# A gated cross-attention layer: the prologue's projections, remainders and bounds in another order

## The reference

```
x = x + tanh(g_xattn) * attention(layernorm(x), ctx, Wq, Wk, Wv, Wo, bo)   # 16 heads of 64
x = x + tanh(g_ffn)  * (layernorm(x) @ W[idx] + b[idx])
q = xn @ Wq ; k = ctx @ Wk ; v = ctx @ Wv
attention = softmax(q @ k.T * 64**-0.5) @ v, heads joined, @ Wo + bo
idx = argmax(log_softmax(logits) - log(-log(u)))     # one of 8 ffn matrices
```

## Time and profile before

| | |
|---|---|
| median of three runs | 1044.47 us |
| profiled execution | 1044.38 us |
| its span, first to last instruction | 1042.6 us |
| granted TensorE clock | full speed over the whole span |
| PE busy | 1027.6 us, 99% |
| DVE busy | 848.2 us, 81% |
| ACT busy | 746.9 us, 72% |
| POOL busy | 442.4 us, 42% |
| between 45 and 88 us: PE, ACT, POOL, DVE busy | 38.49, 37.42, 39.09, 31.66 us of 43 |

### The profile page before, as it was taken

One profiled execution on the slowest core, in us unless ns is written; L12 is line 12 of the kernel. 1 busy time (PEld: TensorE's weight loads), 2 busy tenths in 40 slices (PEclk: granted clock), 3 DMA queues, 4 the chain that ended last, 5 costly groups with the idle time before them and its releaser, 6 DMA issues.

```text
span 1042.6 us, 21852 instructions
## 1 busy us (share of the span) xinstructions
PE 1027.6 (99%) x6074; PEld 587.2 (56%) x6074; DVE 848.2 (81%) x1800; ACT 746.9 (72%) x2720; POOL 442.4 (42%) x637
## 2 busy tenths in 40 slices
PE   9998999999999999999999999999999999999997
PEld 7634455555555555555555555555555555555555
DVE  4678988888888888888888888888888887888876
ACT  3788877777677667776677677776776677767761
POOL 1586344444443344444433344444433344444422
PEclk9999999999999999999999999999999999999999
DMA  8513566666566665665566666655566656655655
GB/s 313 120 31 94 107 124 127 142 123 128 112 133 137 138 136 123 141 128 114 115 135 136 139 135 129 142 119 111 125 137 136 136 129 135 137 119 111 133 107 142
DMA packets 383073, 135.02 MB, mean 130 GB/s; under 512 B 361930, under 2 KB 362750, under 8 KB 382974
## 3 DMA queue, kind: packets, MB, share of 16 engines
q1 hardware_dynamic: 382974, 134.09, 59.4%
HBM read 27.48 MB, written 16.78 MB: 42 GB/s over the span
## 4 chain that ended last, share of the span: by engine, by line
PE 89%; DVE 4%; ACT 3%; DMA 2%; SPq 1%; issue 1%; POOL 0%; DVEq 0%
PE banks L1407 82%; PE banks L1640 3%; ACT work L905 1%; PE banks L1517 1%; DMA fold_area<-in_L_xattn_Wo 1%; PE banks L1453 1%; PE banks L1525 1%; PE banks L1506 1%; DVE fold_area L1124 1%; DVE work L449 1%; ACT vw_area L849 0%; DMA work<-work 0%; DVE vw_area L1113 0%; DVE red L1033 0%; DVE work L1211 0%
## 5 line engine op out<-in xcount | busy, mean ns | idle before, releaser
L905 ACT ACTIVATE work<-banks,red,cst 128x77 f32<-128x77 f32 x1024 | 408.9, 425 | 83.3 <-DVE red L1202 83.2
L1407 PE MATMUL banks<-fold_area,work 128*128 128x456 f16 (+1 forms) x2304 | 405.4, 335 | 2.6 <-DMA work<-work 1.9
L1407 PE MATMUL banks<-vw_area,work 128*128 128x512 f16 x1674 | 371.4, 379 | 1.0 <-DMA work<-work 1.0
L1407 PEld LDWEIGHTS banks<-fold_area,work 128*128 128x128 f16 x2304 | 225.2, 98 | 171.1 <-DMA work<-work 2.7
L1407 PEld LDWEIGHTS banks<-vw_area,work 128*128 128x128 f16 x1674 | 163.6, 98 | 186.1 <-DMA work<-work 1.9
L449 DVE SCALAR_TENSOR_TENSOR work<-work 128x256 f16<-128x256 f32 (+3 forms) x443 | 241.0, 578 | 0.8 <-ACT work L928 0.3
L905 ACT ACTIVATION_READ_ACCUMULATOR work<-banks,red,cst 128x1 f32 x1024 | 219.5, 214 | 0.0
L1200 DVE TENSOR_REDUCE stats<-banks 128x6 f32<-128x462 f32 (+1 forms) x192 | 112.0, 583 | 103.1 <-PE banks L1407 102.7
L1407 PE MATMUL banks<-work 128*128 128x256 f16 x1302 | 162.4, 272 | 0.7 <-DVE work L1287 0.5
L1407 PEld LDWEIGHTS banks<-work 128*128 128x128 f16 x1302 | 126.9, 98 | 31.9 <-DVE work L1287 0.7
L732 POOL TENSOR_TENSOR stats<-stats,cst 128x1 f32<-128x1 f32 x64 | 12.5, 196 | 282.4 <-DVE stats L1236 282.4
(11 more groups left out here) (150 smaller groups left out, 817.8 us busy)
## 6 DMA issues: line engine op xcount, KB each, us to landing
work<-in_x SPq DMA_DIRECT2D x64, 256.0 KB, 2.8
out<-work SPq DMA_DIRECT2D x63, 256.0 KB, 2.2
work<-work SPq DMA_TRANSPOSE x253, 3.1
fold_area<-in_L_xattn_Wo SPq DMA_DIRECT2D x4, 512.0 KB, 9.4
work<-in_L_ffn_W SPq DMA_DIRECT2D x2, 1024.0 KB, 8.3
fold_area<-in_L_xattn_Wq SPq DMA_DIRECT2D x2, 1024.0 KB, 14.2
fold_area<-in_L_xattn_Wv SPq DMA_DIRECT2D x3, 512.0 KB, 6.3
fold_area<-in_L_xattn_Wk SPq DMA_DIRECT2D x2, 768.0 KB, 12.4
```

The lines of the kernel that those rows point to most:

```text
L905: nc.scalar.activation(probs_of(place, place + 1), s_heads(m, k)[:, h - h0, :], ACT.Exp, bias=nmx[:, h:h + 1], scale=exp_scale, accum_out= ...
L1407: mm = nc.tensor.matmul(ps, lhs(l), rhs(r), start=first and n == 0, stop=last and n == 2, skip_group_check=onto)
```

## The change

The order of the visits in the first half of the key phase is another one. All four projections stand first, then two remainders, then the spread and the first turn; KEY 0 to 3 are folded before remainders 2 and 3. From KEY 8 on, and with the same banks, the list is as before. SPREAD becomes two visits: 0 for KK and WQ, 1 for WF. The bounds change engines: of the query matrix, ACT takes the first half in two passes and DVE the second in one reduction; the ffn matrix goes from one reduction on DVE to two passes on ACT. The pieces for x stand at later visits.

```diff
-        FROM = [0, 6, 11, 16, 21]
-        PARTS = [5, 4, 4, 4, 1]
+        FROM = [0, 6, 11, 16, 20]
+        PARTS = [5, 4, 4, 3, 2]
...
-        VISITS = [(PROJECT, 0), (PROJECT, 1), (PROJECT, 2), (REMAINDER, 0), (VALUE, 0), (PROJECT, 3), (REMAINDER, 1), (VALUE, 1),
...
+        VISITS = [(PROJECT, 0), (PROJECT, 1), (PROJECT, 2), (PROJECT, 3), (REMAINDER, 0), (REMAINDER, 1), (SPREAD, 0), (TURN, 0),
+                  (VALUE, 0), (KEY, 0), (KEY, 1), (VALUE, 1), (TURN, 1), (KEY, 2), (KEY, 3), (VALUE, 2), (REMAINDER, 2), (SPREAD, 1),
+                  (KEY, 4), (KEY, 5), (VALUE, 3), (REMAINDER, 3), (TURN, 2), (KEY, 6), (VALUE, 4), (KEY, 7), (VALUE, 5), (PASS, 0), (VALUE, 6),
...
# POOL
-                if (kind, n) == (REMAINDER, 1):
+                if (kind, n) == (KEY, 3):
                     x_scale(0, 0)
-                if (kind, n) == (KEY, 7):
+                if (kind, n) == (KEY, 11):
                     x_scale(0, 1)
...
# ACT
+            def ffn_bounds():
+
+                act.wait_ge(wf_loaded, 16)
+                for n, junk in enumerate((wv_raw[:, CT - 1, :], fold_area[:, A_WORDS + CT * ID:A_WORDS + CT * ID + ID])):
+                    rows = wf_raw[:, n * KT // 2:(n + 1) * KT // 2, :].rearrange("p k n -> p (k n)")
+                    nc.scalar.activation(junk, rows, ACT.Abs, accum_out=part_of(WF, n)).then_inc(parts_ready[WF], 1)
...
             copy_k(0)
+            copy_k(1)
             act.wait_ge(scale_v_ready, 1)
...
                 if t == 0:
-                    act.wait_ge(parts_ready[WF], 1)
+                    act.wait_ge(parts_ready[WF], PARTS[WF])
...
+                if (kind, n) == (PROJECT, 2):
+                    query_bounds()
+                if (kind, n) == (PROJECT, 3):
+                    ffn_bounds()
...
-                if (kind, n) == (VALUE, 2):
+                if (kind, n) == (VALUE, 3):
                     x_normalized(0, 0)
-                if (kind, n) == (REMAINDER, 3):
+                if (kind, n) == (KEY, 6):
                     x_high(0, 0)
...
# DVE
             largest(VV)
+            key_part(0)
             power_of_two(VV, 3)
...
-            dve.wait_ge(wf_loaded, 16)
-            part(WF, 0, wf_raw)
-            largest(WF)
-            key_part(0)
             key_part(1)
...
+                if (kind, n) == (PROJECT, 2):
+                    dve.wait_ge(wq_loaded[1], 16)
+                    part(WQ, 0, wq_raw[:, KT // 2:KT, :])
+                    largest(WQ)
...
-                if (kind, n) == (PROJECT, 3):
+                if (kind, n) == (KEY, 1):
+                    largest(WF)
                     x_moments(0, 0)
                     dve.wait_ge(x_stats, 1)
                     x_variance()
-                if (kind, n) == (KEY, 1):
+                if (kind, n) == (KEY, 7):
                     x_low(0, 0)
...
-                if (kind, n) == (KEY, 4):
+                if (kind, n) == (KEY, 8):
                     x_moments(0, 1)
...
# PE
-                if (kind, n) == (PROJECT, 0):
+                if (kind, n) == (PROJECT, 1):
                     spread(VV, 3)
```

More of the change, by code:

```diff
@@ L364, in flamingo_layer @@
         PROJECT, REMAINDER, VALUE, SPREAD, TURN, KEY, PASS = range(7)
-        VISITS = [(PROJECT, 0), (PROJECT, 1), (PROJECT, 2), (REMAINDER, 0), (VALUE, 0), (PROJECT, 3), (REMAINDER, 1), (VALUE, 1),
-                  (SPREAD, 0), (TURN, 0), (REMAINDER, 2), (VALUE, 2), (REMAINDER, 3), (KEY, 0), (KEY, 1), (VALUE, 3), (TURN, 1),
-                  (PASS, 0), (KEY, 2), (KEY, 3), (VALUE, 4), (PASS, 1), (KEY, 4), (KEY, 5), (VALUE, 5), (TURN, 2), (KEY, 6), (KEY, 7), (VALUE, 6),
+        VISITS = [(PROJECT, 0), (PROJECT, 1), (PROJECT, 2), (PROJECT, 3), (REMAINDER, 0), (REMAINDER, 1), (SPREAD, 0), (TURN, 0),
+                  (VALUE, 0), (KEY, 0), (KEY, 1), (VALUE, 1), (TURN, 1), (KEY, 2), (KEY, 3), (VALUE, 2), (REMAINDER, 2), (SPREAD, 1),
+                  (KEY, 4), (KEY, 5), (VALUE, 3), (REMAINDER, 3), (TURN, 2), (KEY, 6), (VALUE, 4), (KEY, 7), (VALUE, 5), (PASS, 0), (VALUE, 6),
                   (KEY, 8), (KEY, 9), (VALUE, 7), (TURN, 3), (KEY, 10), (KEY, 11), (VALUE, 8), (KEY, 12), (KEY, 13), (VALUE, 9),
@@ L807, in copy_k, with query_bounds @@
                                banks[:, pair_of(PROJECT, n):pair_of(PROJECT, n) + 2, 0:BS]).then_inc(k_copied, 1)
-            def query_bounds(half):
+            def query_bounds():
                 act.wait_ge(floor_set, 1)
-                act.wait_ge(wq_loaded[half], 16)
+                act.wait_ge(wq_loaded[0], 16)
                 act.wait_ge(v_done, HP)
-                for k in (2 * half, 2 * half + 1):
-                    nc.scalar.activation(wv_raw[:, k, :] if k < CT else fold_area[:, A_WORDS + CT * ID:A_WORDS + CT * ID + ID], wq_raw[:, k, :],
-                                         ACT.Abs, accum_out=part_of(WQ, k)).then_inc(parts_ready[WQ], 1)
+                for k in range(KT // 2):
+                    nc.scalar.activation(wv_raw[:, k, :], wq_raw[:, k, :], ACT.Abs, accum_out=part_of(WQ, 1 + k)).then_inc(parts_ready[WQ], 1)
+            def ffn_bounds():
[3 more added lines that the diff above has]
+                    nc.scalar.activation(junk, rows, ACT.Abs, accum_out=part_of(WF, n)).then_inc(parts_ready[WF], 1)
             copy_k(0)
+            copy_k(1)
             act.wait_ge(scale_v_ready, 1)
@@ L871, in _ @@
             for kind, n in VISITS:
-                if kind == PROJECT and n > 0:
+                if kind == PROJECT and n > 1:
                     copy_k(n)
+                if (kind, n) == (PROJECT, 2):
+                    query_bounds()
+                if (kind, n) == (PROJECT, 3):
+                    ffn_bounds()
                 if kind == REMAINDER:
@@ L877, in _ @@
                     value_high(n)
[L878 to L881, removed]
                 if kind == KEY:
@@ L1168, in _ @@
                     key_part(n)
+                if (kind, n) == (PROJECT, 2):
+                    dve.wait_ge(wq_loaded[1], 16)
+                    part(WQ, 0, wq_raw[:, KT // 2:KT, :])
+                    largest(WQ)
                 if (kind, n) == (PROJECT, 3):
                     largest(KK)
-                    largest(WQ)
-                if kind == SPREAD:
+                if (kind, n) == (SPREAD, 1):
+                    power_of_two(WF, pair_of(SPREAD, 1))
+                if (kind, n) == (SPREAD, 0):
                     first = pair_of(SPREAD)
@@ L1179, in _ @@
                                                    op0=ALU.mult, op1=ALU.mult).then_inc(scale_q_ready, 1)
-                    power_of_two(WF, first, P)
-                if (kind, n) == (PROJECT, 3):
+                if (kind, n) == (KEY, 1):
+                    largest(WF)
                     x_moments(0, 0)
@@ L1488, in taken_before @@
                 elif kind == SPREAD:
-                    for m in (KK, WQ, WF):
+                    for m in (WF,) if n else (KK, WQ):
                         pe.wait_ge(pow_step[m], 1)
@@ L1546, in _ @@
                     value_unit(n)
-                if kind == SPREAD:
-                    spread(WF, pair_of(SPREAD), P)
+                if (kind, n) == (SPREAD, 1):
+                    spread(WF, pair_of(SPREAD, 1))
+                if (kind, n) == (SPREAD, 0):
                     spread(KK, pair_of(SPREAD))
```

## The result

| | before | after |
|---|---|---|
| median of 22 runs each, side by side | 1044.01 us | 1045.54 us |
| ratio | | 1.0014, 95% interval 1.0009 to 1.0020 |
| profiled execution / its span | 1044.38 / 1042.6 us | 1045.01 / 1043.2 us |
| KEY 0 folds | 45.42 | 39.92 |
| VALUE 8 folds | 63.77 | 65.06 |

The changed kernel is slower by 1.5 us, 0.14%. The forecast was 1045.4, a change of +1.0. KEY 0 folds 5.5 us earlier, and 25 us later all of it is gone and 1.3 us more. In the profile the exponentials begin 1.29 us later and the spans differ by only 0.6: before's profiled execution had one longer wait for a transpose near its end, 1.20 us where the changed kernel has 0.57. Whether the other executions had it isn't known; their medians differ by 1.5.

A forecast was written before the change was run, and what follows sets the result against it. PE fills 130 to 1000 us, so only its start moves; DVE, POOL and the ffn reload tie the fold phase. 0.0 (POOL) + 0.97 (DVE and ACT) = +1.0 on 1044.38: 1045.4 us, own range 1044.2 to 1046.4, wider range 1042.6 to 1047.2.

The forecast's parts named there:

- What bounds: Whole kernel: PE fills 130 to 1000 us, so only its start moves; no single engine fills the fold phase before.
- The ties of DVE and POOL: End of fold phase: value 7's low half on DVE precedes VALUE 8's fold; POOL's splits run nearly without a gap.
- The reload's: Tie of the ffn matrix, requested when POOL's last value split ends; exponentials follow its two uses, forecast at 92.2 us.
- To the first key fold: Walk from the projections to KEY 0: it folds at 39.55 against 45.42, 5.9 us early, but owed on PE.
- the meeting for x_low: Remainder 3 on POOL: two small subtractions meet DVE's x_low and take 1.39 us; without it the sum is 0.5 smaller.
- POOL: Deciding term: first split 2.3 us late, idle 2.33, remainder 3 ends 59.54, free for VALUE 12 at 75.18; price 0.0.
- The long form of remainder 3's subtractions: POOL's two small subtractions in remainder 3 again take 1.39 us, against 0.94 in remainder 2.
- DVE: Second moments and ACT's wait ahead of value 7's low half: VALUE 8 folds at 64.74 against 63.77, 0.97 us late.
- What I cost at nothing: Moves priced at zero: later x_low(0,0), SP's transposes and bias rows 8 us later, the WF spread and its steps.
- the head start's 1041.9: First rival: ACT's work fills the phase, 5.9 us gained and 3.4 owed, so 2.5 us faster; chance 0.14.
- No change: Second rival: DVE's idle 0.52 and a hardly waiting VALUE 6 copy swallow the moments, 1044.4 us; chance 0.22.
- POOL later than VALUE 12's copy: Third rival: idle before KEY 3 grows, POOL free for VALUE 12 after about 76.2; 1047.2 at 2.8 late; chance 0.16.

The follow-up runs named there:

- e1: Changed kernel with the second tile's moments on DVE behind KEY 6 instead of KEY 8; ratio 1.0011 to the kernel before.
- e2: Changed kernel with remainder 3's split ahead of VALUE 3's split on POOL; ratio 1.0010 to the kernel before.
- e6: Changed kernel with the two remainder stages exchanged, so VALUE 6 shares room with remainders 0 and 2, order unchanged; ratio 1.0009 to the kernel before.
- e4: Kernel before with the second tile's moments behind KEY 8 and its four short POOL instructions behind KEY 11; ratio 1.0002 to the kernel before.
- e5: Kernel before with only the bounds' change of engines, visits as before; ratio 1.0002 to the kernel before.
- e3: Changed kernel with the first tile's moments and POOL's four short instructions back at their old places; ratio 1.0012 to the kernel before.
- e8: Changed kernel with remainder 2 ahead of KEY 0, stages exchanged, first x pieces at old places, second moments, x_low and x_high moved; ratio 0.9994 to the kernel before.

## Why the prediction was right

- *The number*: the mechanism held, the closeness of 1045.4 to 1045.54 is partly luck. The starting point of 1044.38 was 0.37 above the median of 22 runs, and the change was +1.5 against +1.0.
- *What bounds*: the stretch behind 130 us kept its shape and began 1.31 us later, and the exponentials moved with value 7's low half. The ties of DVE and POOL held. The reload's was loose by a hair: its uses ended at 92.34 and DVE's maxima at 92.45, so in the changed kernel the chain runs through the folds.
- *To the first key fold*: forecast 39.55, measured 39.92. One step more than covers the 0.37, the product that makes the query scale. Before it took 0.16 us; now 0.62. It began at 37.75 and ended at 38.37, where POOL's subtraction of the first remainder (37.21, 1.16 long) ended. POOL's first split used to lie elsewhere; I had priced the meeting for x_low and overlooked it here.
- *POOL*: start 36.25 (36.17), idle 2.60 (2.33), remainder 3's end 59.87 (59.54), VALUE 9 69.61 (69.41), VALUE 12 held by ACT and not by POOL. The later places are late by 0.2 to 0.3, KEY 0's 0.37 less some slack. The late first split, which the rivals' paragraph leans on, cost POOL nothing: the idle lay behind it.
- *The long form of remainder 3's subtractions* came again: 1.38 us at 58.09, behind an x_low that had begun at 57.52 and was itself stretched to 1.16. The Trainium skill's rule of the shared port pair (SBUF — State Buffer, "SBUF: two separate sides") agrees with both, and with the 0.62 above. Had I applied it to the product too, the sum would have been near +1.4, an estimate from 0.97 and the 0.46 that the product grew by.
- *DVE*: the term was 0.97, measured 1.29 with that 0.3. Its parts are now measured. Taking the moments away gives 0.71 (e1), taking the wait away 0.9 to 1.1 (e2, e6), together more than the 1.29. They share one path: late KEY 8, moments, KEY 9, value 7. In e6, without the wait, the moments are covered: DVE was done with KEY 9 at 62.36 and ACT's copy of VALUE 7 ended at 62.38. The forecast's sentence "0.82 is the moments' and the rest ACT's wait" gave the division wrongly: without ACT's wait the moments cost 0.18 in the old order (e4) and nothing in e6.
- *What I cost at nothing*: the bounds, rightly (e5). SP's transposes, wrongly argued: "first used at 87.75 by the scores" overlooks that the turned tile also frees the room that x_high(0,1) writes at KEY 17. In the changed kernel the transpose was issued at 70.44 and took 4.5 us, so it landed at 74.9, and x_high ran at 74.98: covered by next to nothing. It cost nothing only because the folds were late too, and that was luck; it gave back much of e1's, e3's and e6's gains. Before, the transpose was issued at 62.33 and x_high ran at 73.61.
- *The rivals*: the head start's 1041.9 is out. What was owed on PE was 5.9 us and what was won 5.5. "No change" is out by the interval. POOL later than VALUE 12's copy didn't happen.

Left open: why the reload's landing time differs between these profiles (5.0 to 5.5 us); where the medians' 1.5 us has the 0.2 that the profile's 1.3 lacks; and whether e8 is truly faster than the kernel before.

## What to carry to other kernels

An engine that starts its part early has won nothing if the work it passed is owed at the same rate: add up, on each engine, what was moved behind. Then follow the engine with the least idle time, here POOL with 39.1 busy of 43 us, by the order of its own queue: a short instruction moved out of its idle place delays everything that shares a buffer with it. And for each buffer that a moved transfer frees, look for every writer, not for the first reader: a cover is as long as the nearest of them. Last, count a gain from a place that the edit can't move, and look which of two waits ended last before calling a gain lost.

## What the runs showed of the hardware

A DVE instruction on one column with two SBUF inputs, 0.15 to 0.16 us by itself, took 0.62 us (after), 0.43 (e6) and 0.85 (e2) beside a POOL subtraction with both inputs in SBUF. Each time it ended with the subtraction, within 0.01 us. In e2 that delayed the first exponentials by 0.70. The moments, an instruction with one input, took 0.68 us with POOL idle (at 38.36 before) and 0.68 beside a POOL subtraction (at 60.79 in e6). The reload of the 1 MB ffn matrix took 5.1 us to land in the changed kernel's profile and 5.5 in those of e1 and e6, where it ended last and the first exponentials began 0.35 and 0.43 us behind DVE's maxima.
